# An attention and ternary FFN block on one core: batches written out, loads split, keys in another bank, one block of the probability cast moved to GpSimd

## The chip, the core and the metric

The kernel runs on one core of a Trainium2 chip. The core has TensorE (PE in the profile), VectorE (DVE), ScalarE (ACT), GpSimd (POOL), SyncE (SP, here used only to start transfers) and 16 DMA engines. The engines run their own instruction streams and meet at semaphores. The metric is the device time of one execution in microseconds (us); lower is better.

## The reference, cut to what matters

For each of B = 2 batches of S = 1024 tokens of width 256:

```
c_kv = x @ w_dkv            # rank 64           c_q = x @ w_dq          # rank 192
k = [rope(x @ w_kr), c_kv @ w_uk]               # 64 + 128 per head, 16 heads
q = [rope(c_q @ w_qr), c_q @ w_uq]              v = c_kv @ w_uv
attn = softmax(q @ k.T / sqrt(192)) @ v         # per head
x = layernorm(x + attn @ w_o)
x = layernorm(x + (silu(x @ w1q.T) * (x @ w3q.T)) @ w2q.T)   # w1q.. are weights rounded to -s, 0, +s
```

The kernel works with absorbed weights: `w_uq @ w_uk.T` and `w_uv @ w_o` are multiplied once at the start, so that each head needs only the 64 latent rows of c_kv as its keys and values, beside the 64 rotary rows.

## The kernel before

**Precision.** Scores and values are products of float16 pairs: every factor is split into a high part (a cast) and a low part (value minus high part), and three products are added. So each matrix is cast by one engine and subtracted by another.

**Start (lines 990 to 1055 for TensorE).** TensorE turns the weights of head h (`turn_weights`), multiplies them (`weight_products`), and turns the product back (`turn_products`). ScalarE copies out of PSUM; VectorE subtracts. With head 8 comes `ff_mean`, a matmul of ones with the absolute sums of w1, w3, w2; it waits for two ScalarE passes over the weights (`absolute_sum`, L512, run with heads 6 and 7) and a VectorE pass. VectorE then makes the ternary weights (L701, L705), TensorE turns them (`turn_ternary`, L1033), and x can be turned (L1063). VectorE ends the stage with a maximum over Wq_hi (L724).

**Batch.** Every engine but SyncE has a hardware loop over the two batches (`Fori(0, B)`). A batch runs: x turned (L1063), projections (L1071), a chain of limits that gives powers of two as scales (L740 to L766), keys (K_hi, K_lo), then the queries (`query_terms`, L1157) in four groups of four tiles, each tile 10 matmuls. Per group VectorE multiplies by the rotary tables (`rotate`, L804), GpSimd adds or subtracts (L398), ScalarE casts, GpSimd makes the low part (L404), and SyncE copies the result into Q_parts with 8 transfers (L329) and 2 more for the latents (L324). SyncE waits for these, loads Wvo_lo and xr (L337, L338, 1 MB each), and starts the transposing transfers (L346).

**Pairs.** The attention itself is PAIRS = 8 pairs of heads, each pair 16 tiles of 128 queries (`TILES`), in two halves of 8. A tile is: scores (L1104, 6 matmuls of 512 columns, in Sa or Sb), maximum (L816, L819), exponent (L582, ScalarE, into one of DEEP = 4 buffers `probs`), and then the 8 blocks of 128 keys go two ways. Two blocks (`KP`) are turned by TensorE (L1115), cast by ScalarE (PT_hi) and subtracted by VectorE (L826). The other six are cast by ScalarE into `P_parts` (part_high, L479, 768 columns), subtracted there by GpSimd (`low_probs`, L426), and transposed by DMA into PT_dma. `P_parts` has 4 buffers too: ScalarE may cast tile n+4 only when the transfer of tile n has landed (`part_in`). The values matmuls (L1133) of one half run beside the scores of the next: two of eight blocks in each step of two tiles. In its first half a batch has no values to do. Once in a half, GpSimd also widens the reciprocals (L411) and splits the output (`low_out`, L418, L420).

The order of the work in one step of two tiles is written out by hand for each engine: `pair_pe`, `pair_act` (exponent n+2, PT_hi, exponent n+3, two casts), `pair_dve`, `pair_pool`, and SyncE's loop at L346.

**Tail.** After the last pair: `project_out` (L1240), the values of the last half, x1 turned (L1253), `hidden` (L1269), `down` (L1283), norms, and the store (L460). GpSimd waits until the store has landed (`y_out`) before it goes to the next batch.

## Time and profile before

| | |
|---|---|
| times of three runs | 957.38, 964.31, 964.38 us; median 964.31 |
| the profiled execution | 965.38 us, span 963.7 us |
| mean granted TensorE clock | 0.969 |
| PE busy | 885.1 us (92%) |
| DVE busy | 668.4 us (69%) |
| ACT busy | 684.6 us (71%) |
| POOL busy | 632.6 us (66%) |
| DMA queue q1 | 422192 packets, 142.91 MB, 72.4% of 16 engines |

The page also has the span in 40 slices of 24.1 us. The slices of the attention stages read 9 for PE and ACT; the first six slices and the ones about the middle do not, and PEclk, the clock that TensorE was granted, drops to 7 in the second slice. Positions in time below are us from the start of the span. The share of PE is a sum of instruction durations that overlap, so it says that TensorE had work, not that it worked at its peak.

### The profile page before, as it was taken

The numbers are of one execution on the slowest core, as the hardware profiler recorded it, in microseconds if no ns is written. First come the engines' busy times: TensorE is split into PE (matmuls) and PEld (weight loads), VectorE is DVE, ScalarE is ACT, GpSimd is POOL, SyncE is SP. The second block draws the span as 40 slices with busy tenths as digits, with TensorE's granted clock in tenths as the row PEclk, the third lists the DMA queues.
The fourth block names the chain that finished last, engine by engine and source line by source line (L and its number), as shares of the span: only waits on it lengthen the run. The fifth ranks groups of instructions, "written<-read, shape, count | busy, mean of one in ns | idle before, by whom it ended". The sixth has DMA issues, their size and how long they took to land.

```text
span 963.7 us, 17672 instructions
## 1 busy us (share of the span) xinstructions
PE 885.1 (92%) x5104; PEld 498.8 (52%) x5104; DVE 668.4 (69%) x1051; ACT 684.6 (71%) x1114; POOL 632.6 (66%) x445
## 2 busy tenths in 40 slices
PE   6979859999999999999988975999999999999985
PEld 3537524444444444458774842444444444446874
DVE  0677747788887878764465873878878887885445
ACT  2553559999999999980333465999999999995132
POOL 0138846787778777872343984787787788777134
PEclk9799979999999999999998997999999999999998
DMA  9663699988888888893501569999888888889201
GB/s 256 175 240 83 153 219 159 166 159 168 166 164 158 169 166 164 158 168 124 191 25 34 120 158 210 169 159 169 166 164 158 168 164 163 161 171 158 86 1 44
DMA packets 422976, 145.87 MB, mean 151 GB/s; under 512 B 407996, under 2 KB 416016, under 8 KB 421904
## 3 DMA queue, kind: packets, MB, share of 16 engines
q1 hardware_dynamic: 422192, 142.91, 72.4%
q0 software_dynamic: 576, 2.10, 0.6%
q8 instruction: 25, 0.41, 0.2%
q10 hardware_dynamic: 160, 0.26, 0.1%
q14 instruction: 23, 0.19, 0.1%
HBM read 23.85 MB, written 7.60 MB: 33 GB/s over the span
## 4 chain that ended last, share of the span: by engine, by line
PE 66%; issue 15%; POOL 8%; DMA 4%; SPq 2%; DVE 2%; ACT 1%; POOLq 0%; ACTq 0%; DVEq 0%
PE Oa L1133 18%; PE Sa L1104 17%; PE Sb L1104 17%; POOL g_lo L455 3%; PE Ta L1115 3%; PE Tb L1115 3%; DMA PT_dma<-P_parts 2%; PE Ob L1143 1%; SPq L346 1%; PE Sb L1240 1%; PE Sa L1157 1%; SPq L329 1%; PE Sb L1157 1%; POOL turned L398 1%; POOL Wq_lo L380 1%
## 5 line engine op out<-in xcount | busy, mean ns | idle before, releaser
L426 POOL TENSOR_TENSOR P_parts<-probs,P_parts 128x768 f16<-128x768 f32 x256 | 417.3, 1647 | 140.3 <-ACT P_parts L479 140.3
L479 ACT ACTIVATE P_parts<-probs 128x768 f16<-128x768 f32 x256 | 202.6, 844 | 21.9 <-DMA PT_dma<-P_parts 21.9
L816 DVE TENSOR_REDUCE nmax<-Sa 128x1 f32<-128x1024 f32 x128 | 156.7, 1224 | 55.7 <-PE Sa L1104 54.8
L582 ACT ACTIVATE probs<-Sa,nmax,scales 128x1024 f32<-128x1024 f32 x128 | 154.1, 1204 | 48.4 <-DVE nmax L819 42.0
L1104 PE MATMUL Sa<-K_hi,Q_parts 128*128 128x512 f16 x512 | 155.4, 385 | 23.9 <-ACT probs L582 23.9
L1104 PE MATMUL Sb<-K_hi,Q_parts 128*128 128x512 f16 x512 | 154.3, 383 | 13.4 <-ACT probs L582 8.4
L816 DVE TENSOR_REDUCE nmax<-Sb 128x1 f32<-128x1024 f32 x128 | 156.1, 1220 | 12.0 <-PE Sb L1104 7.4
L582 ACT ACTIVATE probs<-Sb,nmax,scales 128x1024 f32<-128x1024 f32 x128 | 154.3, 1205 | 1.1 <-DVE nmax L819 1.1
L1133 PE MATMUL Oa<-PT_dma,V_hi 128*64 128x512 f16 x768 | 132.3, 385 | 0.0
L1104 PEld LDWEIGHTS Sa<-K_hi,Q_parts 128*128 (+1 forms) x512 | 40.1, 98 | 105.2 <-issue 45.3
L1104 PEld LDWEIGHTS Sb<-K_hi,Q_parts 128*128 (+1 forms) x512 | 42.9, 98 | 93.8 <-issue 39.0
L826 DVE TENSOR_TENSOR PT_lo<-Ta,PT_hi 128x512 f16<-128x512 f32 x64 | 44.3, 692 | 47.3 <-ACT PT_hi L479 47.0
L1104 PE MATMUL Sa<-K_lo,Q_parts 128*128 128x512 f16 x256 | 77.1, 383 | 0.0
L1104 PE MATMUL Sb<-K_lo,Q_parts 128*128 128x512 f16 x256 | 77.0, 383 | 0.0
L1133 PE MATMUL Oa<-PT_dma,V_lo 128*64 128x512 f16 x384 | 73.4, 379 | 0.0
L1133 PEld LDWEIGHTS Oa<-PT_dma,V_hi 128*64 128x64 f16 x768 | 43.1, 109 | 45.2 <-issue 14.7
L826 DVE TENSOR_TENSOR PT_lo<-Tb,PT_hi 128x512 f16<-128x512 f32 x64 | 44.3, 691 | 25.5 <-ACT PT_hi L479 24.9
L819 DVE TENSOR_SCALAR nmax<-nmax,scales 128x1 f32<-128x1 f32 x256 | 54.9, 214 | 9.0
L455 POOL TENSOR_TENSOR g_lo<-QO,g_hi 128x512 fp32r<-128x512 f32 x24 | 31.5, 1318 | 37.0 <-ACT g_hi L479 37.0
L420 POOL TENSOR_TENSOR O_parts<-QO,O_parts (+1 forms) x32 | 40.7, 1273 | 6.0 <-POOL O_parts L418 6.0
L398 POOL TENSOR_TENSOR turned<-qmul 128x1024 f32<-128x1024 f32 x16 | 38.0, 2396 | 5.7 <-DVE qmul L804 5.7
L1115 PE MATMUL Tb<-ident,probs 128*128 128x128 f32 x256 | 39.3, 275 | 2.1 <-ACT probs L582 2.1
(303 smaller groups left out, 1537.9 us busy)
## 6 DMA issues: line engine op xcount, KB each, us to landing
Q_parts<-turned_parts SPq DMA_DIRECT2D x64, 128.0 KB, 2.4
TT<-ternary SPq DMA_DIRECT2D x2, 2304.0 KB, 8.6
Q_parts<-Q_parts SPq DMA_DIRECT2D x16, 256.0 KB, 3.0
PT_dma<-P_parts SPq DMA_TRANSPOSE x256, 3.9
ternary<-tern SPq DMA_DIRECT2D x1, 2304.0 KB, 7.7
wo<-in_L_attn_w_o_dram SPq DMA_DIRECT2D x4, 512.0 KB, 8.6
xq<-in_L_attn_x_dram SPq DMA_DIRECT2D x2, 1024.0 KB, 12.6
wq_low<-Wq_lo SPq DMA_DIRECT2D x1, 2048.0 KB, 14.2
```

Of the source, the lines that this page charges most:

```text
L398: nc.gpsimd.tensor_tensor(turned[:, j, :], qmul[:, 2 * j, :], qmul[:, 2 * j + 1, :], op).then_inc(rope_sum, 1)
L420: nc.gpsimd.tensor_tensor(O_parts[:, pair_row + 1, cols], QO[:, pair_row + 1, cols], O_parts[:, pair_row, cols].bitcast(F), ALU.subtract). ...
L426: nc.gpsimd.tensor_tensor(P_parts[:, n % DEEP, 1, :], probs[n % DEEP][:, KP * P:S], P_parts[:, n % DEEP, 0, :], ALU.subtract).then_inc(par ...
L455: nc.gpsimd.tensor_tensor(g_lo[:, t, :], gate[:, t % 2, :], g_hi[:, t, :].bitcast(F), ALU.subtract).then_inc(glo_done, 1)
L479: return nc.scalar.activation(o, i, ACT.Copy, scale=scale)
L582: nc.scalar.activation(probs[n % DEEP], SS[n % 2][:, :], ACT.Exp, bias=nmax[:, n % 4:n % 4 + 1], scale=score_down, accum_out=den[:, n // 8 ...
L816: nc.vector.tensor_reduce(nmax[:, n % 4:n % 4 + 1], SS[n % 2][:, :], AX.X, ALU.max, negate=True).then_inc(row_max, 1)
L819: nc.vector.tensor_scalar(nmax[:, n % 4:n % 4 + 1], nmax[:, n % 4:n % 4 + 1], score_down, PROB_UP_LOG, ALU.mult, ALU.add).then_inc(max_rea ...
L826: nc.vector.tensor_tensor(PT_lo[place].rearrange("p k (t q) -> p t k q", t=2), TS[n // 2 % 2][:, :].rearrange("p (t k q) -> p t k q", t=2, ...
L1104: last = mm(bank[:, m * HALF:(m + 1) * HALF], Q_parts[:, p * 2 + a, part, q:q + P], c[:, m * HALF:(m + 1) * HALF], start=(k == 0), stop=(k ...
L1115: last = nc.tensor.transpose(TS[n // 2 % 2][:, at:at + P], probs[n % DEEP][:, k * P:(k + 1) * P], ident[:, :])
L1133: last = mm(Oa[64 * a:64 * a + 64, :], v[:, k, :], pt[:, a, :], start=(k == 0 and i == 0), stop=(k == KT - 1 and i == 2))
```

## The change

1. **Batches written out.** The hardware loops over B on TensorE, VectorE, ScalarE and GpSimd become Python loops; the loops over pairs stay.
2. **Start.** 24 transposes of the identity (`WARM`) run on TensorE before the weights arrive. `ff_mean` is at head 9 instead of 8, and ScalarE's `absolute_sum` comes after `weights_out`.
3. **Keys in another bank.** Oa and Ob become one tensor OO; the key projection goes there, so that Sa is free for the first query tile. The query terms wait for cq_hi and cq_lo only; the keys are awaited before the fourth query tile. The sign of one rotary product is put into its scale (`k_minus`), so GpSimd needs one addition of 64 rows instead of two of 32.
4. **Rotary low part.** For groups 0 to 2, the low part of the odd rows moves from GpSimd to VectorE.
5. **SyncE.** Wvo_lo and xr are loaded in four pieces, before pairs 1, 2, 4 and 6. SyncE no longer waits for the query copies before the first transposing transfer.
6. **Pairs.** The first of six blocks is cast by GpSimd. `reciprocal` moves behind the two maxima, `row_out` ahead of PT_lo.
7. **Tail.** `project_out` is split into early and late parts in another order.

```diff
+WARM = 24
@@ SyncE
-                        sp.wait_ge(rope_lo, b * 2 * GROUPS + 2 * g + j + 1)
+                        sp.wait_ge(rope_lo[j], b * GROUPS + g + 1)
...
-                for j in range(2):
-                    sp.wait_ge(turned_out[j], (b + 1) * 64 * GROUPS)
-                sp.wait_ge(q_ps, (b + 1) * 4 * GROUPS)
-                sp.wait_ge(wq_out, 16)
-                sp.wait_ge(wvo_out, 16)
-                sp.dma_start(Wvo_lo[:, :, :]..., wvo_low).then_inc(wvo_in, 16)
-                sp.dma_start(xr[:, :, :], x_v[b]).then_inc(xr_in, 16)
-                with sp.Fori(0, PAIRS) as p:
+                def pair_sp(p, first):
...
+                def prefetch(c):
+                    part = slice(2 * c, 2 * c + 2)
+                    sp.dma_start(Wvo_lo[:, part, :]..., wvo_low[:, 2 * c * D:(2 * c + 2) * D]).then_inc(wvo_in, 16)
+                    sp.dma_start(xr[:, part, :], x_v[b][:, part, :]).then_inc(xr_in, 16)
+                pair_sp(0, True)
...
+                for c, end in enumerate((2, 4, 6, PAIRS)):
+                    prefetch(c)
+                    with sp.Fori(max(1, end - 2), end) as p:
+                        pair_sp(p, False)
@@ GpSimd
-            with pool.Fori(0, B) as b:
+            for b in range(B):
...
-                nc.gpsimd.tensor_tensor(kmul[0:32, :], kmul[0:32, :], kturn[0:32, :], ALU.subtract).then_inc(k_rot, 1)
-                nc.gpsimd.tensor_tensor(kmul[32:64, :], kmul[32:64, :], kturn[32:64, :], ALU.add).then_inc(k_rot, 1)
+                nc.gpsimd.tensor_tensor(kmul[0:64, :], kmul[0:64, :], kturn[0:64, :], ALU.add).then_inc(k_rot, 1)
...
-                    for j in range(2):
+                    for j in range(2 if g == GROUPS - 1 else 1):
...
                     hold(pool, part_hi, tile + 1)
+                    nc.gpsimd.tensor_copy(P_parts[:, n % DEEP, 0, 0:P], probs[n % DEEP][:, KP * P:(KP + 1) * P]).then_inc(part_cast, 1)
+                    hold(pool, part_cast, tile + 1)
                     nc.gpsimd.tensor_tensor(P_parts[:, n % DEEP, 1, :], probs[n % DEEP][:, KP * P:S],
                                             P_parts[:, n % DEEP, 0, :], ALU.subtract).then_inc(part_lo, 1)
@@ ScalarE
-                if h in (6, 7):
-                    absolute_sum(h - 5)
                 if h + 2 < H:
                     weights_out(h + 2)
+                if h in (6, 7):
+                    absolute_sum(h - 5)
...
-                scaled(K_hi[64:128, :], Sa[64:128, :], k_up[64:128]).then_inc(k_lat_hi, 1)
                 scaled(cq_hi[:, :], Sb[:, :], cq_up).then_inc(cq_hid, 1)
                 ... (cq_s)
+                scaled(K_hi[64:128, :], OO[64:128, :], k_up[64:128]).then_inc(k_lat_hi, 1)
...
-                    copy(P_parts[:, n % DEEP, 0, :], probs[n % DEEP][:, KP * P:S]).then_inc(part_hi, 1)
+                    copy(P_parts[:, n % DEEP, 0, P:KD * P], probs[n % DEEP][:, (KP + 1) * P:S]).then_inc(part_hi, 1)
@@ VectorE
+                key_product(slice(0, 64), slice(0, 64), kmul, k_up, tcos)
                 ... (cq_lo, cq_s low)
+                key_product(slice(32, 64), slice(0, 32), kturn, k_up, tsin)
+                key_product(slice(0, 32), slice(32, 64), kturn, k_minus, tsin)
+                ... (K_lo of the latents)
+                def rotary_parts_low(g):
+                    dve.wait_ge(rope_hi, b * 2 * GROUPS + 2 * g + 2)
+                    if g >= 1:
+                        dve.wait_ge(turned_out[1], b * 64 * GROUPS + 64 * g)
+                    nc.vector.tensor_tensor(turned_parts[:, 1, 1, :], turned[:, 1, :], turned_parts[:, 1, 0, :],
+                                            ALU.subtract).then_inc(rope_lo[1], 1)
                 for g in range(GROUPS):
                     rotate(g)
                     latents_low(g, 0)
+                    if g:
+                        rotary_parts_low(g - 1)
...
-                            if not (first and h == 0):
-                                reciprocal(pair * 2 + h - 1, 1 - h)
                         ... (two maxima)
-                        transposed_low(pair * (TILES // 2) + n // 2, n + 1)
+                        if n % 8 == 0 and not (first and h == 0):
+                            reciprocal(pair * 2 + h - 1, 1 - h)
                         if n % 8 == 2 and not (first and n == 2):
                             row_out(pair * 2 + n // 8 - 1)
+                        transposed_low(pair * (TILES // 2) + n // 2, n + 1)
@@ TensorE
+            for _ in range(WARM):
+                nc.tensor.transpose(SQ[3][:, 0:P], ident[:, :], ident[:, :])
...
-                if h == 8:
+                if h == 9:
                     ... (ff_mean)
-                project((SQ[0], SQ[1]), lambda kc: wkv[:, kc, :], 1).then_inc(kv_ps, 1)
+                project((Oa, Ob), lambda kc: wkv[:, kc, :], 1).then_inc(kv_ps, 1)
...
-                pe.wait_ge(k_mul, b * 3 + 3)
-                pe.wait_ge(k_lat_lo, b + 1)
+                pe.wait_ge(lim_step, b * LSTEPS + 1)
                 pe.wait_ge(cq_hid, b * 3 + 1)
-                query_terms(0, 0, (0,))
+                query_terms(0, 0, (0, 2))
...
+                pe.wait_ge(k_mul, b * 3 + 3)
+                pe.wait_ge(k_lat_lo, b + 1)
                 query_terms(0, 3, range(5))
...
-                project_out((0, 1))
+                project_out((0, 1), early)
                 sums_to_rows(group)
-                project_out((2, 3))
+                project_out((2, 3), early)
+                project_out((0, 1, 2, 3), late)
                 for k in range(KT):
                     values(group, 1, k)
+                project_out((4, 5), early)
                 turn_x1(0)
-                project_out((4, 5))
-                project_out((6, 7))
+                project_out((6, 7), early)
+                project_out((4, 5, 6, 7), late)
```

## Rows read from the trace of the kernel before

**Rows 1.** The page, part 4: the chain that ended last, shares of the span.
```profile
PE 66%; issue 15%; POOL 8%; DMA 4%; SPq 2%; DVE 2%; ACT 1%; POOLq 0%; ACTq 0%; DVEq 0%
```

**Rows 2.** Windows: length, then PE, PEld, DVE, ACT, POOL busy, clock, DMA share, GB/s.
```profile
7.30:24.30 17.00, 16.99 (x56) 9.12 (x56) 2.36 (x6) 4.72 (x13) 0.00 (x0) 1.00 1.08 296
30.40:41.40 11.00, 10.94 (x38) 5.97 (x38) 6.22 (x12) 3.66 (x11) 0.00 (x0) 0.53 0.74 221
41.40:52.00 10.60, 9.55 (x64) 6.66 (x63) 9.65 (x12) 9.21 (x22) 8.55 (x5) 1.00 0.06 26
137.60:143.50 5.90, 5.82 (x16) 2.60 (x17) 2.61 (x4) 4.48 (x8) 4.07 (x3) 0.50 1.15 162
183.50:221.90 38.40, 38.07 (x234) 17.87 (x233) 31.02 (x47) 35.70 (x57) 30.74 (x22) 1.00 0.91 168
```

**Rows 3.** Timeline of the start: start us, us, engine, line, op [idle before <-releaser].
```profile
0.84 0.20 POOL L364 MEMSET ident<- 128x128 f32 x1 [0.29 <-POOLq L1324]
...
10.79 0.48 PE L998 MATMUL Ta<-ident,wuq_a 128*128 128x128 f32 x1
...
27.58 0.33 PE L998 MATMUL Tb<-ident,wuq_a 128*128 128x128 f32 x1
...
30.46 0.36 PE L1043 MATMUL Sb<-asum,ones 128*128 128x3 f32 x2 [0.90 <-ACT below L512]
```

**Rows 4.** Timeline of the keys of batch 0 and the start of batch 1.
```profile
65.62 1.11 ACT L551 ACTIVATE cq_hi<-Sb,scales 128x1024 fp32r<-128x1024 f32 x1
66.36 1.27 DVE L777 SCALAR_TENSOR_TENSOR kturn<-Sa,scales,tsin 32x1024 f32<-32x1024 f32 x1
70.50 0.73 PE L1157 MATMUL Sa<-cq_hi,Wq_hi 128*128 128x512 f32 x2 [3.34 <-DVE K_lo L780]
...
503.09 1.11 PE L1063 MATMUL Oa<-ident,xq 128*128 128x128 f32 x4 [2.90 <-issue]
...
511.03 0.20 POOL L384 MEMSET ones_b<- 128x128 f32 x1 [4.01 <-DMA out_dram<-QO]
```

**Rows 5.** Timeline of the first pair of a batch, SyncE's queue, ACT and PE.
```profile
124.27 0.34 SPq L337 DMA_DIRECT2D Wvo_lo<-wvo_low  x1
125.58 5.73 SPq L346 DMA_TRANSPOSE PT_dma<-P_parts  x1
134.18 0.84 ACT L479 ACTIVATE P_parts<-probs 128x768 f16<-128x768 f32 x1 [8.28 <-DMA PT_dma<-P_parts]
137.68 1.03 PE L1104 MATMUL Sa<-K_hi,Q_parts 128*128 128x512 f16 x2 [9.82 <-ACT probs L582]
...
589.92 1.03 PE L1104 MATMUL Sa<-K_hi,Q_parts 128*128 128x512 f16 x2 [10.71 <-ACT probs L582]
```

**Rows 6.** Groups by line: count | busy us, mean ns | idle before, releaser.
```profile
L426 POOL TENSOR_TENSOR P_parts<-probs,P_parts 128x768 f16<-128x768 f32 x256 | 417.3, 1647 | 140.3 <-ACT P_parts L479 140.3
L479 ACT ACTIVATE P_parts<-probs 128x768 f16<-128x768 f32 x256 | 202.6, 844 | 21.9 <-DMA PT_dma<-P_parts 21.9
...
L418 POOL CAST O_parts<-QO (+1 forms) x32 | 19.5, 610 | 5.8 <-DVE QO L844 5.8
```

**Rows 7.** Timeline of one half of a pair in the steady stage.
```profile
211.08 1.27 POOL L420 TENSOR_TENSOR O_parts<-QO,O_parts  x1 [0.19 <-POOL O_parts L418]
212.31 4.85 POOL L426 TENSOR_TENSOR P_parts<-probs,P_parts 128x768 f16<-128x768 f32 x3
214.05 1.43 SPq L346 DMA_TRANSPOSE PT_dma<-P_parts  x1
217.49 1.58 ACT L479 ACTIVATE P_parts<-probs 128x768 f16<-128x768 f32 x2
217.75 0.60 PE L1104 MATMUL Sb<-K_hi,Q_parts 128*128 128x512 f16 x2
```

**Rows 8.** The transposing transfers from 200 to 240 us, issue to landing.
```profile
DMA to landing us min/median/max: 3.6/3.8/4.0
```

**Rows 9.** Timeline of the tail of batch 0, the first output projection.
```profile
436.29 0.50 PE L1240 MATMUL Sa<-Wvo_hi,O_parts 128*128 128x256 f32 x2 [0.78 <-POOL O_parts L420]
```

131 lines of the change are left out of this document (69 added, 62 removed).

## The prediction, made before the kernel was built

> **What bounds the kernel now.** I read the chain of waits first: TensorE holds 66% of it [rows 1], so I looked for stretches in which TensorE waits or runs slowly, and for what limits it where it does neither. The windows give the second. A pair of heads in the steady stage takes 38.4 us, with TensorE busy 38.07 of them and ACT 35.70, DVE 31.02, POOL 30.74 [rows 2]: 14 of the 16 pairs are TensorE's, and a faster cast by ACT gains nothing there. The timeline gives the first, four places. **Start:** the same transpose takes 0.48 us at 10.79 and 0.33 us at 27.58 [rows 3]; the second slow stretch, 30.40 to 41.40, is granted 0.53, half the 2.4 GHz, after TensorE had waited for `ff_mean` [rows 2, 3]. (The clock column says 1.00 in the first stretch, where the durations do not; I go by durations.) **Keys:** TensorE waits until 70.50 for K_lo, though cq_hi was ready at about 66.7 [rows 4]. **First pair:** TensorE stands still for 9.82 us in batch 0 and 10.71 in batch 1, and then runs at 0.50 for 5.90 us [rows 5, 2]. Read upwards: ACT waits 8.28 us for the landing of the first transposing transfer, which sits behind the 2 MB of Wvo_lo and xr issued from 124.27, and which also blocked SyncE for 5.73 us. **Between batches:** 2.90 us of issue at the loop's turn [rows 4].
>
> The profiled execution took 965.38 us (span 963.7), 1.1 above the median of 964.31; the sum is made against 965.4.
>
> **The change, part by part.**
>
> *Start.* At full clock a slow stretch takes 0.33/0.48 = 0.69 of its time or less. The first (17.00 us) would give 5.3, the second (11.00) 3.4, the wait for `ff_mean` 0.9 [rows 2, 3]: 9.6. A bound from DVE agrees: its work between `ff_mean` and the turning of x is 6.22 + 9.65 = 15.9 us of the 21.6 [rows 2]; it can give up at most 5.7 us there, and the rest must come ahead of `ff_mean`. DVE then sets the end, TensorE waits for ternary weights, and may fall to the slow level again. I take 8, between 3.5 (only the wait and half the second stretch) and 10.5. The 24 transposes themselves cost nothing: TensorE has nothing to do before its first weights.
>
> *Keys and queries.* TensorE can start the queries once cq_s's projections are through, some 4 us earlier; the keys move behind on DVE (two products of 1.27 us and K_lo [rows 4]) and are done before the fourth tile needs them. One GpSimd addition instead of two, and one rotary subtraction per group fewer on GpSimd. VectorE gets 3 subtractions of 1024 columns, 1.27 us each if they cost what its product of that width does, beside the 40 matmuls that TensorE has in a group. Gain 4 per batch, and 1 more in the limits chain where the projection of x no longer stands ahead of the sums: 9 in all, bounds 5 and 13. In batch 1 the 2.90 us of the loop are free, but `ones_b` is set only at 511.03, after the store has landed [rows 4], and that is not moved: I count 1 of the 2.90 there.
>
> *First pair.* With the 2 MB gone and SyncE free of the waits, the first transfer starts when its low part is ready, some 4 us after ACT casts, and lands 3.8 later [rows 8]. ACT then waits perhaps 1.5 us for it. Gain: 9.82 + 10.71, and half of the two slow stretches of 5.90 (2.7 each, 5.4), less 2 x 1.5: 23. Lower bound 15 (if the query copies now ahead of it in the queue cost as much again as half of the wait), upper 26. ACT's cast of 640 instead of 768 columns saves some 0.12 of its 844 ns [rows 6]; only in the four steps of the first half, where ACT is the bound, does that count: 4 x 2 x 0.12 x 2 batches = 2, and I take 1.
>
> *The prefetch pieces.* 512 KB each, four a batch. The 2 MB cost the first transfer about 4.8 us of landing (8.6 from 125.58 to 134.18, against 3.8 [rows 5, 8]), so a piece costs a quarter, 1.2, up to 2. They come between pairs, where the next tile's buffer has 2 us to spare. 8 x 0.4 = 3 lost; bounds 0 and 12.
>
> *The cast on GpSimd.* This is the part that works against the change. Its price is in no row. Nearest below is a 128-column memset, 0.20 us [rows 3]; above, half of the 512-column cast, 0.31 [rows 6]. I take 0.21, nearer to the row of equal width. The subtraction must wait for the cast: 0.19, as between L418 and L420 [rows 7]. So 0.40 per tile, 3.2 us per half of 8 tiles, on top of 30.74/2 = 15.4: 18.6 of 19.2. POOL goes from 80% to 97%. It hangs on a ring: the fourth subtraction of a half ends at 213.92, its transfer is issued at 214.05, lands at 217.85 [rows 7, 8], and ACT wants that buffer at about 218.2, for the second of the casts from 217.49. There is 0.35 us to spare. Three casts lie in front of it since GpSimd last waited, 1.0 us with the reciprocal that now comes 1 us later; so ACT will wait 0.65 to 1.0 us there once in every half, its next exponent is late, and the scores after it, for which TensorE already waits (0.28 us before 217.75), come later by 0.3 net. 30 halves x 0.3 = 9 lost. Bounds: 0 (cast at 0.20 without the wait) and, with 0.31, 19.5 us of POOL work in a half, 0.7 x 30 = 21.
>
> [...]
>
> *Tail.* The 0.78 us wait [rows 9] goes, but rows 4 to 7 of the residual now all finish after the last projection, so x1 of the second half comes about 1.5 us later for TensorE. Loss 1.5 in all, bounds -2 and 4.
>
> **Sum.** 965.4 - 8 - 9 - 1 - 23 - 1 + 3 + 9 + 1.5 = 936.9. Against the median, 936.
>
> **The rivals.**
> *No toll in the pairs:* the ring absorbs the cast. For it: DMA to landing never exceeds 4.0 us, and POOL's sum is below the period. Against it: 0.35 us of slack. It gives 937 - 9 - 3 = 925.
> *The start and the queue give little:* the 24 transposes don't lift the clock and the stage waits for DVE, and the first transfers are late behind query copies. 937 + 4.5 + 8 = 949. For it: DVE is busy 9.65 of 10.60 us before x is turned. Against it: the stretch 41.40 to 52.00, whose later part is transposes alone, keeps 1.00 [rows 2], so transposes hold the clock.
> The Trainium skill (TensorE: Matmul & The Clock Gate, Part 4: PE-mode transpose) says that the full clock does not engage for transposes. By that rule the warm-up would do nothing and only this rival's first half holds; the row just named speaks against it.
> *GpSimd becomes the bound (slower than before):* the cast and its wait take 0.75 us a tile, say because GpSimd and DVE hinder each other. Then a half needs 15.4 + 8 x 0.75 = 21.4, 2.2 over 19.2, 66 us in 30 halves against 42 gained and 4.5 lost elsewhere: 965.4 - 37.5 + 66 = 994. It decides from 37.5/30 = 1.25 us a half, 15.4 + 8c = 20.45, c = 0.63 us a tile. Against it: no POOL row of this width comes near.
> *The loops:* written-out code waits for its instructions, each first pass as at 503. That would be some 3 us at a few places, within the range.
>
> **Chances.** Forecast (930 to 945) 0.5; no toll (918 to 930) 0.2; little at start and queue (945 to 956) 0.18; gains eaten by a toll of 1 us or more per half (956 and up) 0.12, of which above 974 0.05. The range leaves out the last and the best tail: 921 to 954. What a measurement of this kernel can tell from no change is about 1%, so faster means below 954.7: 0.87; within 1% 0.08; slower 0.05.
>
> **What the profile after would show.** Start: x turned at 42 to 45 instead of 52, L998 at 0.33 from the first head. Keys: first L1157 at about 58. Pair 0: no wait of TensorE over 2 us. Steady pair: 38.4 becomes 39.0, POOL at 36 to 37, and ACT P_parts waits for DMA about once a half; if it stays at 38.4, the toll is wrong; if it is over 40, POOL's cast was under-priced. The forecast is wrong as a whole if the wait of 9.82 comes back elsewhere in pair 0, above all behind the query copies.

## The result: 0.8% faster, just above the range

The changed kernel takes 954.28 us (median of 13 runs, 951.11 to 958.70), the kernel before in the same rounds 962.01 (957.38 to 966.02). The ratio is 0.9922, interval 0.9902 to 0.9942: some 7.5 us faster where 26 to 29 were forecast. The range was 921 to 954, so the median lies 0.3 us above it. The direction was right and the size was not. The profiled execution took 958.38 us (span 956.5), 4 above its median; the one of before, 965.38, stood 3.4 above its own. One profile used below, e3's, is of a slow run (984.28 us, its median 976.15), so only its stretches are used, beside medians of all runs.

The page of the changed kernel, part 4, the chain that ended last, and three groups of part 5 (count | busy us, mean ns | idle before, releaser), which answer to [rows 1, 6]:
```profile
PE 20%; issue 6%; ACT 4%; DVE 4%; POOL 3%; DMA 3%; POOLq 0%; ACTq 0%; DVEq 0%; SPq 0%
...
L439 POOL TENSOR_TENSOR P_parts<-probs,P_parts 128x768 f16<-128x768 f32 x256 | 420.8, 1644 | 46.6 <-POOL P_parts L437 46.6
L492 ACT ACTIVATE P_parts<-probs 128x640 f16<-128x640 f32 x256 | 182.5, 736 | 50.2 <-DMA PT_dma<-P_parts 49.6
...
L437 POOL CAST P_parts<-probs 128x128 f16<-128x128 f32 x256 | 74.2, 290 | 14.3 <-ACT P_parts L492 14.3
```
The subtraction on GpSimd waited 140.3 us for ScalarE before; it now waits 46.6 for its own engine's cast. ScalarE's wait for the ring rose from 21.9 to 50.2 us. Both rows say the same: GpSimd has fallen behind and ScalarE runs into it. (The chain in the first line could be followed back to 552 us only, its shares add to 43%, and it can't be set beside the one of [rows 1].)

Windows of the changed kernel: two halves of a steady pair, and the stretch of the start with the low clock (length, then PE, PEld, DVE, ACT, POOL busy, clock, DMA share, GB/s):
```profile
243.54:283.31 39.77, 38.23 (x233) 17.86 (x232) 30.64 (x47) 34.03 (x56) 35.02 (x39) 1.00 0.89 171
...
10.00:20.80 10.80, 10.80 (x37) 5.80 (x37) 1.60 (x4) 3.02 (x9) 0.00 (x0) 0.53 1.09 299
```
Beside the row of 38.40 us in [rows 2] the pair is 1.37 us longer. TensorE's work is the same, GpSimd's has grown from 30.74 to 35.02, and no engine is busy for the whole of it.

Where the time went, by the starts of the same TensorE instructions in the two traces (us, batch 0 / batch 1; x turned, first query, first scores, first rows turned, last rows turned):

| stretch | before | changed |
|---|---|---|
| to x turned, batch 0 | 52.0 | 46.1 |
| x turned to first query | 18.5 / 19.3 | 13.8 / 18.8 |
| first query to first scores | 37.3 / 36.8 | 35.7 / 35.7 |
| first scores to first rows turned | 44.3 / 44.7 | 40.0 / 39.1 |
| first to last rows turned (15 halves) | 284.9 / 284.9 | 292.8 / 292.2 |
| last rows to the next x, or to the end | 66.0 / 74.9 | 66.8 / 75.5 |

("Rows turned" is the widened reciprocal turned by TensorE, once in a half.) 23.8 us were won ahead of and in the first pairs, the pairs behind gave back 15.2 of them and the tails 1.4. Below, "half" is the mean of 22 steady halves, 11 of each batch: 19.18 before, 19.87 changed.

### The profile page after: what moved, and what is told of

It reads as the page before. It is cut to its first block and busy times, and to the rows that moved or that the text cites. A ratio compares the mean times of both kernels' runs of the same rounds, so it can differ in the third digit from the quotient of the medians.

```text
span 956.5 us, 17395 instructions
## 1 busy us (share of the span) xinstructions
PE 886.4 (93%) x5128; PEld 499.0 (52%) x5128; DVE 671.4 (70%) x1059; ACT 659.8 (69%) x1113; POOL 684.3 (72%) x693
## 5 line engine op out<-in xcount | busy, mean ns | idle before, releaser
L439 POOL TENSOR_TENSOR P_parts<-probs,P_parts 128x768 f16<-128x768 f32 x256 | 420.8, 1644 | 46.6 <-POOL P_parts L437 46.6
L492 ACT ACTIVATE P_parts<-probs 128x640 f16<-128x640 f32 x256 | 182.5, 736 | 50.2 <-DMA PT_dma<-P_parts 49.6
L1161 PE MATMUL OO<-PT_dma,V_hi 128*64 128x512 f16 x768 | 132.3, 385 | 0.0
L1132 PEld LDWEIGHTS Sb<-K_hi,Q_parts 128*128 (+1 forms) x512 | 42.5, 98 | 99.4 <-issue 42.6
L437 POOL CAST P_parts<-probs 128x128 f16<-128x128 f32 x256 | 74.2, 290 | 14.3 <-ACT P_parts L492 14.3
L1161 PE MATMUL OO<-PT_dma,V_lo 128*64 128x512 f16 x384 | 73.4, 379 | 0.0
L1161 PEld LDWEIGHTS OO<-PT_dma,V_hi 128*64 128x64 f16 x768 | 43.1, 109 | 45.2 <-issue 14.4
L851 DVE TENSOR_TENSOR PT_lo<-Ta,PT_hi 128x512 f16<-128x512 f32 x64 | 44.2, 690 | 24.8 <-ACT PT_hi L492 24.7
```

The lines of the kernel that those rows point to most:

```text
L437: nc.gpsimd.tensor_copy(P_parts[:, n % DEEP, 0, 0:P], probs[n % DEEP][:, KP * P:(KP + 1) * P]).then_inc(part_cast, 1)
L439: nc.gpsimd.tensor_tensor(P_parts[:, n % DEEP, 1, :], probs[n % DEEP][:, KP * P:S], P_parts[:, n % DEEP, 0, :], ALU.subtract).then_inc(par ...
L492: return nc.scalar.activation(o, i, ACT.Copy, scale=scale)
L851: nc.vector.tensor_tensor(PT_lo[place].rearrange("p k (t q) -> p t k q", t=2), TS[n // 2 % 2][:, :].rearrange("p (t k q) -> p t k q", t=2, ...
L1132: last = mm(bank[:, m * HALF:(m + 1) * HALF], Q_parts[:, p * 2 + a, part, q:q + P], c[:, m * HALF:(m + 1) * HALF], start=(k == 0), stop=(k ...
L1161: last = mm(Oa[64 * a:64 * a + 64, :], v[:, k, :], pt[:, a, :], start=(k == 0 and i == 0), stop=(k == KT - 1 and i == 2))
```

## The experiments

All times are medians; the kernel before had 960.6 to 963.0 us beside them, so the ratios are compared, and "by the ratios" takes their difference times 962 us.

| run | what differs | us | ratio, 95% interval | half |
|---|---|---|---|---|
| changed | | 954.28 | 0.9922 [0.9902, 0.9942] | 19.87 |
| e1 | changed, casts on ScalarE | 934.95 | 0.9729 [0.9686, 0.9771] | 19.18 |
| e2 | changed, reciprocal first | 941.42 | 0.9785 [0.9742, 0.9828] | 19.37 |
| e3 | changed, loads first | 976.15 | 1.0128 [1.0076, 1.0181] | 20.03, one of 22.91 in it |
| e4 | changed, no transposes at the start | 955.05 | 0.9929 [0.9902, 0.9956] | 19.86 |
| e5 | before, with the cast | 971.63 | 1.0087 [1.0054, 1.0119] | 19.40, one of 20.98 in it |
| e15 | changed, cast of 64 columns | 948.32 | 0.9846 [0.9804, 0.9888] | 19.75 |
| e16 | changed, ScalarE casts all six as well | 957.48 | 0.9956 [0.9922, 0.9991] | 19.98 |
| e13 | e1, reciprocal first | 934.95 | 0.9720 [0.9681, 0.9759] | 19.18 |
| e6 | e1, one subtraction behind the maximum | 934.07 | 0.9705 [0.9668, 0.9742] | 19.18 |
| e7 | e1, batches in loops | 938.19 | 0.9744 [0.9707, 0.9780] | 19.18 |
| e8 | e1, keys first | 943.46 | 0.9796 [0.9757, 0.9835] | 19.18 |
| e9 | e1, last rotary subtraction on GpSimd | 932.91 | 0.9692 [0.9659, 0.9726] | 19.19 |
| e10 | e1, all of them on GpSimd | 935.39 | 0.9717 [0.9679, 0.9755] | 19.19 |
| e11 | e1, ff_mean as before | 939.22 | 0.9760 [0.9726, 0.9794] | 19.25, one of 20.56 in it |
| e12 | e1, tail as before | 932.86 | 0.9702 [0.9665, 0.9739] | 19.19 |
| e14 | e1 + e9 + e12 | 927.62 | 0.9641 [0.9598, 0.9684] | 19.18 |

### The toll in the pairs

**e1, all casts on ScalarE.**
```diff
-copy(P_parts[:, n % DEEP, 0, P:KD * P], probs[n % DEEP][:, (KP + 1) * P:S])
+copy(P_parts[:, n % DEEP, 0, :], probs[n % DEEP][:, KP * P:S])
-nc.gpsimd.tensor_copy(P_parts[:, n % DEEP, 0, 0:P], ...).then_inc(part_cast, 1)
-hold(pool, part_cast, tile + 1)
```


> The changed kernel, with one edit: ScalarE casts all six blocks of probabilities again and GpSimd only subtracts. In the changed kernel a steady half of a pair takes 19.66 to 20.02 us where it took 19.11 to 19.20 before. Theory GpSimd is full: per half it subtracts 8 times (8 x 1.64), casts 8 times (8 x 0.29), waits for its own cast 8 times (8 x 0.18), casts and subtracts 256 columns of heads, widens, and waits 0.5 us for the reciprocal, some 19.8 us in all, which is the half. Then without the cast and its wait (3.8 us of each half) the half goes back to 19.1 to 19.3 us, and 28 to 30 halves give 14 to 20 us back: about 937 us. Theory of the transfers (the pieces of the loads between pairs, or the ring's landings, stretch the half): the halves stay at 19.7 us or more and the time within 4 us of 954. Theory of the moved reciprocal and row copy: likewise no change here.

934.95 us, the half at 19.18 as before the change. The ratio falls by 0.0193, 18.6 us: the cast on GpSimd costs that much, and not the pieces of the loads, which are still between the pairs. The toll is this one edit's, but the waits show that not all of it is its work. GpSimd's waits in this kernel (total us, times, longest):
```profile
POOL P_parts L437 <- ACT P_parts L490: 92.0, 68, 1.8
...
POOL rden_wide L422 <- DVE rden L856: 28.0, 30, 1.0
```
GpSimd waits 0.93 us a half for the late reciprocal, almost twice as long as in the changed kernel (15.1 us in 30 times), and the half is the shortest there is.

**e2, the reciprocal ahead of the maxima.** In the order of VectorE:
```diff
+if n % 8 == 0 and not (first and h == 0): reciprocal(...)
 maximum(t0 + n + 2, n + 2)
 maximum(t0 + n + 3, n + 3)
-if n % 8 == 0 and not (first and h == 0): reciprocal(...)
```


> The changed kernel, with one edit: VectorE takes the reciprocal of a half's sums before the two maxima again, as in the kernel before, so that GpSimd need not wait 0.5 us a half for it (15.1 us in 30 waits). Theory GpSimd is full: every us that it does not wait shortens the half, until the half reaches 19.2 us; 30 halves x 0.5 give 12 to 15 us, so 939 to 942 us. Theory of latency (the half is longer since each tile's cast delays the landing in the ring, and GpSimd has slack elsewhere): under 3 us.

941.42 us, 13.2 less by the ratios, the half 19.37. GpSimd no longer waits for it at all. So 0.49 of the 0.68 us of a half hang on the place of an instruction for which the prediction's sum has no term of its own.

**e13, e1 with the reciprocal first**, the fourth corner:

> The changed kernel without the cast on GpSimd and with the reciprocal ahead of the maxima: the fourth corner beside the changed kernel (954.28), the one without the cast (934.95) and the one with the early reciprocal (941.42). Theory that the late reciprocal costs only where GpSimd is full: steady halves stay at 19.19 us, and the time is 934 to 936. Rival, that the late reciprocal costs about the same 0.4 us a half with and without the cast, hidden so far: some us less, under 931.

934.95 us against e1's 934.95. Without the cast the late reciprocal is free; with it, it costs 13.

**e5, the cast alone on the kernel before**, the same two edits as e1 turned round.

> The kernel before, with one part of the change: GpSimd casts the first 128 columns of each tile's probabilities and ScalarE the other five blocks. Nothing else is moved; the reciprocal comes before the two maxima. With that order the changed kernel's half took 19.38 us on the mean, with the later reciprocal 19.86, and without the cast 19.19. Theory that cast and late reciprocal add up on a full GpSimd: here a half takes 19.3 to 19.45, 28 steady halves cost 4 to 7 us, and the time is 3 to 7 us above the kernel before. The rival, that the whole toll of 0.67 us a half belongs to the cast (the reciprocal only shifts where GpSimd waits): 19.8 or more, 15 to 20 us above.

971.63, 8.4 us slower, interval 5.2 to 11.4. Its steady halves are 19.33 but for one of 20.98, so 0.15 x 28 = 4.2 us come from the steady halves. The rest of this execution's stands in two neighbouring halves of the second and third pair of batch 0 (20.29 and 20.98, 2.9 us; why there stays open) and in the last half of each batch (17.4 in place of 16.6, 1.6 us). The size lies just above what was expected; the rival's 15 to 20 are excluded.

**e15, a cast of 64 columns**, ScalarE casting the other 704.
```diff
-P_parts[:, n % DEEP, 0, 0:P]
+P_parts[:, n % DEEP, 0, 0:64]
```


> The changed kernel, with GpSimd casting 64 columns of each tile and ScalarE the other 704. A GpSimd cast takes 0.29 us for 128 columns and 0.61 for 512, so some 0.24 for 64: 0.05 less, 0.4 us in a half. Theory that GpSimd's time is the half: 19.86 becomes 19.4 to 19.5 us, 30 halves give 11 to 13 us, 941 to 943. Rival, that it is the wait for its own cast (0.18 us, unchanged) and the delay of the landing: under 3 us, 951 or more.

948.32, 7.3 us less by the ratios (the halves account for 3 of them, and the intervals leave room for that), the half 19.75: neither of the two. The groups of this kernel:
```profile
L492 ACT ACTIVATE P_parts<-probs 128x704 f16<-128x704 f32 x256 | 195.1, 789 | 38.0 <-DMA PT_dma<-P_parts 35.7
L437 POOL CAST P_parts<-probs 128x64 f16<-128x64 f32 x256 | 61.0, 238 | 23.4 <-ACT P_parts L492 23.3
```
The cast fell by 52 ns as it should, 0.42 us a half; the half fell by 0.11, and GpSimd's wait for ScalarE grew by 9 us. GpSimd's work is not the half by itself. What the edit took off GpSimd it put on ScalarE (736 to 789 ns), so I looked for a cycle through both. The changed kernel's steady half, GpSimd, then ScalarE (start us, us, engine, line, op [idle before <-releaser]):
```profile
255.59 0.61 POOL L429 CAST O_parts<-QO  x1
256.39 1.27 POOL L431 TENSOR_TENSOR O_parts<-QO,O_parts  x1 [0.19 <-POOL O_parts L429]
257.60 0.29 POOL L437 CAST P_parts<-probs 128x128 f16<-128x128 f32 x1
258.07 1.65 POOL L439 TENSOR_TENSOR P_parts<-probs,P_parts 128x768 f16<-128x768 f32 x1 [0.18 <-POOL P_parts L437]
...
268.17 0.29 POOL L437 CAST P_parts<-probs 128x128 f16<-128x128 f32 x1 [0.23 <-ACT P_parts L492]
268.64 1.64 POOL L439 TENSOR_TENSOR P_parts<-probs,P_parts 128x768 f16<-128x768 f32 x1 [0.18 <-POOL P_parts L437]
270.80 0.62 POOL L422 TENSOR_SCALAR rden_wide<-rden 128x512 f32<-128x512 f32 x1 [0.52 <-DVE rden L858]
```
```profile
263.79 0.74 ACT L492 ACTIVATE P_parts<-probs 128x640 f16<-128x640 f32 x1 [1.29 <-DMA PT_dma<-P_parts]
...
267.27 1.36 ACT L492 ACTIVATE P_parts<-probs 128x640 f16<-128x640 f32 x2
```
The subtraction that ends at 259.72 releases the transfer that lands 3.9 us later; at 263.79 ScalarE, which has waited 1.29 us for it, goes on; two exponents, a copy and two casts later GpSimd gets the tile for which it has waited 0.23 us at 268.17; and from there its four tiles, the wait for the reciprocal, the widening and the two steps for O_parts lead to the next half's 259.72 + 19.9. That closes. The late reciprocal stands in this cycle with its whole 0.52 us: without it the cycle would take 19.35, and e2's half is 19.37. The cycle holds four casts of GpSimd (0.052 less each in e15) and two of ScalarE (0.053 more each): 0.10 less, and 0.11 was measured. Both sums were made after the runs.

**e16, the first block cast twice**, by ScalarE and then by GpSimd over it (only the first line of e1's diff).

> The changed kernel, with ScalarE casting all six blocks of each tile (0.844 us in place of 0.736) and GpSimd still casting the first block over it. GpSimd's work is that of the changed kernel to the nanosecond. With 64 columns on GpSimd its work fell 0.42 us a half, but the half only 0.11 (19.86 to about 19.75), so GpSimd's time alone does not set it. Theory of a cycle, read from the changed kernel's steady half: GpSimd's four tiles with the wait for the reciprocal, the widening and the heads' parts between them (about 11.4 us, from the wait on ScalarE at 248.3 to the subtraction that ends at 259.7), the transfer (3.9 us, landing at about 263.7), then on ScalarE three casts, two exponents and a copy to 268.1, where GpSimd waits for the cast: 19.8 us. It holds three of ScalarE's casts, so here it grows by 3 x 0.11 = 0.3 us: a half of 20.15 us, 28 to 30 halves, 8 to 10 us more, 963. Theory that GpSimd's work alone sets the half: 19.86 and 954 to 955.

957.48, 3.3 us more by the ratios (the intervals overlap), the half 19.98, so 0.11 longer with GpSimd's work unchanged (its cast 290 ns, its subtraction 1644). Theory "GpSimd alone" had none of that; the cycle had 0.3, with three casts of ScalarE in it. The rows above show two, 2 x 0.107 = 0.21, and the wait for the reciprocal fell from 0.52 to 0.41, so 0.10 are left. So the expectation had miscounted the casts and held that wait constant. The cycle fits e2, e15 and e16 to 0.02 us, but only its sign was said ahead of a run.

### The first pair and the queue

**e3, the loads and the waits ahead of the first pair again** (the pieces kept):
```diff
+for j in range(2): sp.wait_ge(turned_out[j], (b + 1) * 64 * GROUPS)
+... (waits for q_ps, wq_out, wvo_out), then for c in range(4): prefetch(c)
 pair_sp(0, True)
-for c, end in enumerate((2, 4, 6, PAIRS)): prefetch(c); with sp.Fori(max(1, end - 2), end) as p: ...
+with sp.Fori(1, PAIRS) as p: pair_sp(p, False)
```


> The changed kernel, with one edit: the loads of Wvo_lo and of the rows (still in four pieces each) and the waits for the turned keys and queries stand ahead of the first pair on SyncE again. The predicted gain of the first pair was 11.5 us a batch; from the first query to the first output projection the changed kernel gained only 6.4 and 7.1 us, once 14 halves x 0.67 us are taken off. If this edit carries that gain, it gives it back: 12 to 15 us more, about 967 us, with a wait of TensorE of 8 to 11 us in the first pair of each batch, and steady halves as in the changed kernel. If the pieces between pairs are what stretches the steady half (theory of the transfers), halves go back to 19.2 us, which gives 19 us, and the sum is about 948 us.

976.15, 19.8 us more by the ratios, where 12 to 15 were expected. From the first scores to the first rows it takes 50.3 and 49.6 us against 40.0 and 39.1. The two rows that answer to [rows 5], in its batch 1:
```profile
595.64 0.74 ACT L494 ACTIVATE P_parts<-probs 128x640 f16<-128x640 f32 x1 [8.15 <-DMA PT_dma<-P_parts]
```
```profile
599.05 1.04 PE L1134 MATMUL Sa<-K_hi,Q_parts 128*128 128x512 f16 x2 [9.60 <-ACT probs L596]
```
The hole is back, so the queue's order is what removes it. But 10 us a batch is more than the 4.4 and 5.7 by which the stretch shortened from the kernel before, since e3 is not that kernel. Its batch 0:
```profile
116.87 0.35 SPq L349 DMA_DIRECT2D Wvo_lo<-wvo_low  x1
...
121.23 19.13 SPq L343 DMA_TRANSPOSE PT_dma<-P_parts  x8
```
The first scores start at 95.97 there and at 107.82 before. The first load is issued 20.9 us behind them (before 16.5), and the first transposing transfer, after eight issues instead of two, 25.3 us behind them (before 17.8 [rows 5]). So e3 shows what carries the gain and overstates its size.

How large it is, the landing of that transfer tells. The changed kernel, batch 0:
```profile
101.85 1.20 ACT L594 ACTIVATE probs<-Sa,nmax,scales 128x1024 f32<-128x1024 f32 x1 [3.83 <-issue]
...
108.01 5.00 SPq L330 DMA_DIRECT2D Q_parts<-turned_parts  x8
113.22 16.85 SPq L343 DMA_TRANSPOSE PT_dma<-P_parts  x8
...
117.96 0.74 ACT L492 ACTIVATE P_parts<-probs 128x640 f16<-128x640 f32 x1 [0.71 <-DMA PT_dma<-P_parts]
119.99 0.74 ACT L492 ACTIVATE P_parts<-probs 128x640 f16<-128x640 f32 x1 [1.29 <-DMA PT_dma<-P_parts]
```
and the kernel before, the first exponent of batch 0 and the wait for the transfer in batch 1:
```profile
111.35 1.21 ACT L582 ACTIVATE probs<-Sa,nmax,scales 128x1024 f32<-128x1024 f32 x1 [2.25 <-DVE nmax L819]
...
586.42 0.84 ACT L479 ACTIVATE P_parts<-probs 128x768 f16<-128x768 f32 x1 [9.17 <-DMA PT_dma<-P_parts]
```
Counted in us from the first scores (batch 0 / batch 1):

| | before | changed |
|---|---|---|
| first exponent starts | 3.5 / 3.5 | 6.2 / 7.6 |
| first low part ends | 12.6 / 12.6 | 15.8 / 17.2 |
| first transposing transfer issued | 17.8 / 17.8 | 17.6 / 18.8 |
| it has landed | 26.3 / 27.2 | 22.3 / 22.7 |

The transfer goes out no sooner than before. It still stands behind the last query copies in SyncE's queue, and its low part comes 3.2 and 4.6 us later, 0.47 of that for GpSimd's cast and its wait and the rest for a later first exponent. What is won is the landing: 4.0 and 4.5 us sooner, since the 2 MB are not ahead of it (from issue to landing 4.7 us in batch 0; 8.6 before, 7.3 in e3). In the changed kernel TensorE then waits elsewhere, batch 1:
```profile
558.79 0.59 PE L1132 MATMUL Sa<-K_hi,Q_parts 128*128 128x512 f16 x2 [3.94 <-ACT probs L594]
563.27 1.03 PE L1132 MATMUL Sb<-K_hi,Q_parts 128*128 128x512 f16 x2 [2.41 <-ACT probs L594]
```
Seven more waits of 0.2 to 1.3 us follow, all for an exponent.

**e6, e9, e10: VectorE's rotary subtractions.** The rotary step stands ahead of the first maximum in the changed kernel, VectorE:
```profile
98.77 1.61 DVE L811 TENSOR_TENSOR turned_parts<-turned,turned_parts 128x1024 f16<-128x1024 f32 x1
100.30 1.21 DVE L841 TENSOR_REDUCE nmax<-Sa 128x1 f32<-128x1024 f32 x1
```
The scores it takes its maximum of were done at 97.1. In e6 it moves behind that maximum, in e9 and e10 it (or all three a batch) goes back to GpSimd:
```diff
-if g: rotary_parts_low(g - 1)                         # VectorE
+if g and g < GROUPS - 1: rotary_parts_low(g - 1)      # e6, e9; e10: none
+rotary_parts_low(GROUPS - 2)                          # e6: after the first maximum
-for j in range(2 if g == GROUPS - 1 else 1):          # GpSimd
+for j in range(2 if g >= GROUPS - 2 else 1):          # e9; e10: range(2)
```


> The changed kernel with all casts on ScalarE (934.95 us), and one step moved: VectorE takes the last of the rotary subtractions that the change gave it (1.61 us) behind the maximum of the first tile, not ahead of it. In the changed kernel the scores of tile 0 are done at 97.1, the maximum starts at 100.30, the first exponent at 101.85 with an idle time of ScalarE put down to issue (3.83 us), and TensorE waits 2.55 us at 103.29 (2.58 and 3.96 us in the kernel with all casts on ScalarE). Theory that the subtraction ahead is what holds them: 1.4 to 1.6 us less in each batch, some 3 us in all, about 932 us. Rival, that ScalarE waits for its instructions or its table there: nothing, 935 us, and the idle time of 3.8 us stays.

> The changed kernel with all casts on ScalarE (934.95 us), with one of the three rotary subtractions a batch that VectorE took over, the last, on GpSimd again. From the first scores to the first turned rows it took 38.6 and 39.3 us there, where the prediction needed some 33; moving that subtraction only behind the first maximum gave nothing (38.9 and 39.4), since the second maximum still stood behind it. Theory that VectorE's 1.61 us delay both maxima, and with them ScalarE's first two exponents: 1.5 us less in each batch, 932. Rival: GpSimd's own 2.1 us for it then delay the last turned queries, and so the first low parts and transfers: 0 to 2 us more.

> The changed kernel with all casts on ScalarE (934.95 us), with all rotary subtractions on GpSimd as before. From the first query to the first scores the kernel before took 37.3 and 36.8 us, the changed one 35.7 in both batches. Theory that this 1.1 to 1.6 us come from the moved subtractions: here 37 again, and 1.5 us less after the first scores, so the time is the same within 1 us. Rival (the 35.7 come from the keys being out of the way, the subtractions give nothing): 35.7 stays, and the stretch after the first scores is 1.5 us shorter: 932.

e6: 934.07, no difference from e1. ScalarE's idle time ahead of its first exponent went from 3.91 to 2.30 us, as the first theory said, but the second maximum is still behind the 1.61 us, and TensorE's wait moved there (Sb, up to 5.1 us). e9: 932.91; from scores to rows 37.6 us in batch 1 where e1 has 39.3; batch 0 (40.0) ran through a stretch at the low clock. e10: 37.2 and 37.6 us, while the 35.7 from query to scores become 35.8 and 35.9. So these subtractions won nothing where they were taken from, and cost 1.5 us a batch where they were put. That is read from the traces; the totals of e9 and e10 differ from e1's by less than their intervals.

What is then left in the first pair, from a window of e10 at full clock, first scores to first rows:
```profile
540.66:578.21 37.55, 26.33 (x131) 12.70 (x131) 26.54 (x39) 31.48 (x50) 29.15 (x18) 1.00 0.88 170
```
ScalarE is busy 31.48 of 37.55 us and TensorE 26.33, so TensorE is not the bound here. Nor is any other engine alone: the chain that ended last in this window has 21.9% in issue, 18.5% in SyncE's starting of transposing transfers, 10.6% in their landing and 9.8% in exponents.

**e8, the keys ahead of the queries** (ScalarE's K_hi, VectorE's three products and K_lo, and TensorE's waits for them, all ahead of the first query; the bank kept).

> The changed kernel with all casts on ScalarE (934.95 us), with the keys ahead of the queries again: ScalarE scales the latent half of K, VectorE forms all three products of the keys and K_lo before cq_lo, and TensorE waits for the keys before its first query. By the prediction (4 us a batch) this gives 8 us back: 943. By the traces (from x turned to the first query 18.5 and 19.3 us before; 13.8 and 18.9 in the changed kernel) the first batch gained 4.7 and the second 0.4, so if nothing else hides it here: 5 us, 940. If the order costs nothing since another wait takes its place, 935 to 936.

943.46, 6.4 us more by the ratios; TensorE waits for K_lo again:
```profile
61.88 0.71 PE L1183 MATMUL Sa<-cq_hi,Wq_hi 128*128 128x512 f32 x2 [3.13 <-DVE K_lo L794]
...
507.94 0.70 PE L1183 MATMUL Sa<-cq_hi,Wq_hi 128*128 128x512 f32 x2 [1.10 <-DVE K_lo L794]
```
x turned to first query is 16.9 and 20.5 us (13.2 and 18.8 in e1), and first query to first scores 37.3 in batch 0. The order of the keys is worth 5 to 6 us by these stretches.

### Start, loops, tail

**e4, WARM = 0.**

> The changed kernel, without the 24 transposes that TensorE does first of all. The start (to x turned, 46.11 us after, 51.98 before) gained 5.9 us. If the transposes bring the granted clock up earlier and carry that, x is turned 3 to 6 us later and the time is 3 to 6 us longer. If transposes do nothing for the clock (as the Trainium skill has it in TensorE: Matmul & The Clock Gate, on what counts as activity), the time is the same within 1 us or up to 1 us shorter, and the 5.9 us come from the other edits of the start.

955.05 against 954.28: nothing. First transposes of the weights, without and with the 24 (the second fence is the changed kernel):
```profile
7.19 0.45 PE L1023 MATMUL Ta<-ident,wuq_a 128*128 128x128 f32 x1 [7.19 <-DMA wuv<-in_L_attn_w_uv_dram]
```
```profile
1.69 5.18 PE L1062 MATMUL Sb<-ident 128*128 128x128 f32 x24 [1.69 <-POOL ident L380]
7.36 0.30 PE L1023 MATMUL Ta<-ident,wuq_a 128*128 128x128 f32 x1 [0.49 <-DMA wuv<-in_L_attn_w_uv_dram]
```
The 24 transposes do lift the clock. Of the 24, with nothing else on TensorE, the first takes 0.47 us, the next 21 take 0.42 and the last two 0.32 and 0.27; the transpose behind them is at 0.30, as at the 2.4 GHz level. Without them the same instruction is at 0.45 to 0.48 until 10.68 and at 0.33 from 12.90. The Trainium skill (TensorE: Matmul & The Clock Gate, Part 4: PE-mode transpose) says that full clock does not engage for transposes. These rows disagree with it for the f32 transposes of this kernel. But the lift saves next to nothing: x is turned at 41.62 without them and at 41.08 with them in e1, where TensorE then waits 0.21 and 0.69 us for loads (at 8.55 and 19.95) for which it does not wait without them.

**e11, ff_mean one head earlier and the absolute sum ahead of the weights' copy, as before.**

> The changed kernel with all casts on ScalarE (934.95 us), with ff_mean one head earlier on TensorE and the absolute sum ahead of the copy of the weights on ScalarE, as before. x was turned at 51.98 before, at 41.1 to 42.7 in runs of the changed kernel whose start had the full clock, and at 44.0 to 46.3 in those with a slow stretch in it. Without the 24 transposes it was 41.62. Theory that this order (a wait of 0.90 us, and the slow stretch of 11 us behind it) carries most of the start's gain: x turned 4 to 9 us later, 939 to 943 us. Rival, that the gain comes from elsewhere (the banks of x, the chance of a slow stretch): under 1.5 us.

939.22, 3 us more by the ratios, the intervals overlap. The total is at the edge of what was expected, but not by the way expected: the wait of 0.90 us is back, and no slow stretch stands behind it. The profiled execution had one from 10 to 16 us, and x turned at 45.0. With the start as changed, x was turned between 41.1 and 51.1 us in 14 profiled kernels, 44.2 on the mean. The five without a slow stretch had it at 41.1 to 42.7, the nine with one at 42.6 to 51.1. The latest, e10:
```profile
22.82 0.47 PE L1019 MATMUL Ta<-ident,wuq_a 128*128 128x128 f32 x1 [2.76 <-DMA wuv<-in_L_attn_w_uv_dram]
```
```profile
23.00:42.00 19.00, 19.00 (x63) 10.46 (x64) 7.90 (x16) 8.79 (x21) 0.00 (x0) 0.50 0.92 243
```
TensorE had waited 2.76 us for weights that landed late, and then ran 19 us without a gap at 1.2 GHz. The changed kernel waited 0.60 us for `wo` at 9.17 and was slow until 20, e3, e8 and e11 waited 0.87, 1.10 and 0.61 us at the same place and were slow behind it, while e1 waited 0.21 there and kept the full clock. But the length of the wait does not decide it: e15 waited 0.61 us and e10 1.37 at that place, e6 2.02 at 21.6, and none of them was slow behind it. So each slow stretch in these starts has a wait ahead of it, and what else decides is open. The start's gain varies from execution to execution by that, and the median holds a mixture. Whether the order of ff_mean carries a part of it, this run does not settle. Its 0.90 us was followed by full clock this once, while in e9 and e14, which have the new order, TensorE waited 1.33 and 1.10 us for the same sum and was slow behind it.

**e7, the batches in loops.**

> The changed kernel with all casts on ScalarE (934.95 us), with the two batches in a loop again on ScalarE, VectorE, GpSimd and TensorE. Theory of the prediction: the loop's turn costs TensorE 2.9 us at the start of batch 1, but only about 1 us of it is on the path, since the sums wait for ones_b: 1 us more, 936. Rival 1: written-out code waits for its instructions in places where the loop does not, so the loops are 1 to 3 us faster. Rival 2: the turn is paid in full and in several engines one after the other: 3 us or more slower.

938.19, not to be told from e1 by the intervals. TensorE again waits for issue at the turn, 2.40 and 2.75 us, but from the turning of x1a, the first half of x1, in batch 0 to the first query of batch 1 it takes 68.0 us against 68.4 in e1. The turn is hidden. One thing is the other way round: with loops ScalarE loads its table at the turn (481.54), written out it does so ahead of the first exponent of batch 1 (the changed kernel):
```profile
556.06 1.28 ACT L594 ACT_TABLE_LOAD   x1 [3.80 <-issue]
```
From first scores to first rows batch 1 takes 37.8 us with loops and 39.3 in e1. That is rival 1 in part, 1.5 us; the total doesn't show it, since this run's start lost 2.9 us to a slow stretch (x turned at 44.0).

**e12, the output projection in the order before.**

> The changed kernel with all casts on ScalarE (934.95 us), with the output projection in the order before. The prediction has the new order cost 1.5 us in all: then 933.5. By the traces the last half of pairs takes 14.83 us and not 16.59, and from its turned rows to the next batch's x 66.6 and not 66.0: a gain of 1.1 us a batch, so 937 here.

932.86, 2.6 us less by the ratios, again within the intervals; the trace is clearer. Last turned rows to the next x:
```profile
412.53:476.79 64.26, 61.05 (x406) 52.09 (x405) 31.80 (x71) 18.32 (x30) 21.47 (x18) 0.97 0.32 111
```
66.6 us in e1; the last half is 15.61 in place of 14.83. The new order loses 1.5 us a batch. The prediction's sign holds and its size (1.5 in all) is doubled; my expectation from comparing before with e1 was wrong in sign, since other edits shorten the last half as well.

**e14, e1 with e9's and e12's edits.**

> The parts of the change that paid, together: all casts on ScalarE, the last rotary subtraction of a batch on GpSimd, the output projection in the order before, all the rest as in the changed kernel. Alone the last two gave 2.0 and 2.1 us beside 934.95, by the traces 1.7 us in a batch (37.6 us from the first scores to the first turned rows) and 1.6 us in a batch (the last half and the tail). If they add up: 931 us, at most 932. If one hides the other, 933.

927.62, 3 below what was expected, 0.9641 of the kernel before and 8.5 us below e1 by the ratios; the traces explain about 6 of these (1.7 and 1.5 a batch). It is the fastest of all: 27 us below the changed kernel.

## Why the prediction was wrong

Two steps failed, the price of the toll in the pairs (18.6 us for 9) and the size of the first pair (10 us for 23).

**Cast on GpSimd.** The prediction saw "the reciprocal that now comes 1 us later" and let it go into the slack of one ring buffer, with no term of its own. In fact it sits in the cycle that the cast had closed, and costs 13 of the 18.6 us (e1, e2, e13); without the cast it costs nothing. A second size was off too. "I take 0.21, nearer to the row of equal width": the cast takes 0.290. The wait of 0.19 is 0.18. The nearest row by width was a memset, which reads nothing; half of the cast of 512 columns was 0.31 and nearly right. But this mis-sizing alone is not the toll: with the early reciprocal the half grew by 0.19 (e2) or 0.15 (e5), less than the 0.3 predicted, and the cast alone cost 6 to 8 us where 9 were forecast.

The upper bound of 21 held, by luck: it stands on 0.7 us a half, while the 19.5 us of GpSimd's work named beside it are only 0.3 over 19.2. What "would show" it is a weak sign as well: a pair of 39.0 was forecast and over 40 would have meant an under-priced cast; it is 39.77, with the cast under-priced by 0.08 us.

**First pair.** Predicted 23 us, measured 4.4 + 5.7 by the stretches. The mechanism was right: putting the loads back brings the hole back (e3). Three parts of the sum were not:

- The gain was taken from TensorE's waits of 9.82 and 10.71 us, where the chain's own wait was ScalarE's, 8.28 [rows 5] and 9.17. TensorE was not the bound of that stage, and when its long wait went, others for exponents came (2.41 to 3.94 us, five of them over 2 in the two batches).
- The first transfer was to start when its low part is ready. It starts 1.8 and 1.6 us later than that, behind the query copies, and the low part itself comes 3.2 and 4.6 us later than before. Of the first exponent's 2.7 us in batch 0, some 1.5 are the rotary subtraction that the same change put in front of the first maximum (6.2 us behind the first scores, 4.7 in e9 and e10), which the prediction counted only beside the queries; 1.2 stay open. In batch 1 a table load of 1.3 us is added.
- 5.4 us were counted for the slow stretches behind the waits. They went in part only: the mean granted clock from the first scores to the first rows is 0.85 and 0.89 before, 0.91 in both batches of the changed kernel.

ScalarE's waits account for the rest, a sum made after the runs. Batch 0: 8.28 less the 0.71 and 1.29 that it still waits and less 1.6 for the subtraction leaves 4.7, measured 4.4. Batch 1: 9.17 less 0.64, 1.6 and 1.3 leaves 5.6, measured 5.7. The forecast's test for it, "no wait of TensorE over 2 us in pair 0", failed.

**Start.** 8 predicted, 7.8 on the mean of 14 profiles, 5.9 in this one. The 24 transposes lift the clock, as argued from the stretch before x was turned, and carry no time (e4): TensorE then arrives sooner at weights that have not landed. "L998 at 0.33 from the first head" held in e1; in the profile of the changed kernel it held for two heads. That the sum of the start came out may be luck, since its largest part, 5.3 us for the first slow stretch, rested on the transposes; what carries the gain in its place was not isolated.

**Keys and queries.** 9 predicted, 7.9 by the stretches (4.7 + 0.5, and 1.6 + 1.1), but 6.3 of them in batch 0; in batch 1 the sums hold the start, and TensorE waited only 1.10 us for the keys when they were put back.

**Pieces, loops, tail.** The pieces: 3 predicted, nothing: e1 has them between its pairs and its half is 19.18. Loops: 1 predicted, none shown. Tail: 1.5 lost predicted, 3 by e12's trace.

The difference to the forecast, in us: the toll 18.6 for 9 (+10), the first pairs 10 for 23 (+13), keys (+1), loops and ScalarE's shorter cast, not seen (+2), the pieces (-3), last half and tail, 1.4 gained for 1.5 lost (-3), and the base, an execution 3.4 above the median of these rounds (-3): 936.9 + 17 = 954. The forecast gave 945 to 956 a chance of 0.18, as the case that start and queue give little. The time fell there in part by luck: the start gave its 8, the toll is no part of that case, and of the 13 us that the first pairs fell short the query copies, its mechanism, show under 2 a batch.

## What to carry to other kernels

When work is added to an engine (here GpSimd went from 80% busy to 88% of a steady pair, and with the waits for its own casts to some 95%), price again every late operand of it, above all those that the same change moves: alone the late reciprocal cost nothing and the cast 6 to 8 us, together 19. Size the end of a stall by the wait of the engine that carries the stage, not by that of the engine with the longest wait. And price an operation by the row of the same operation at another width, not by another operation of the same width.

## What the runs showed of the hardware

- A GpSimd cast from f32 to f16 took 238 ns for 64 columns and 290 for 128: 0.8 ns a column on some 190 ns. The cast of 512 columns [rows 6] took 610; its output is fp32r where the trace gives the form, and it lies near the same line (602). A dependent instruction on the same engine came 0.18 us after it.
- Every stretch in these starts in which the granted clock fell to 0.5 followed a wait of TensorE, the shortest 0.60 us. In the longest TensorE ran at that level without a gap for 19 us. Not every wait was followed by one: e6 waited 2.02 us at 21.6 and kept 1.00.
- 24 f32 transposes, with no other work on TensorE, raised its clock: they began at 0.42 us each and the last took 0.27.
- VectorE's last rotary subtraction of a batch took 1.61 us in the changed kernel and 1.21 in e6, the same form at another moment. Which neighbour slows it was not tried.
- Written out, ScalarE's table load moved from the batch's start to its first exponent: same 1.28 us, another place.
